# LayerNorm statistics taken block by block on ScalarE, and half of the prologue's transposes evicted by it

## What is computed

```
x = x + LN(attention(LN(x)))          # 32 query heads, 8 key/value heads, D = 128, causal
x = x + LN(ffn(LN(x)))                # base linear 4096 x 4096 + bias + 8 LoRA experts, top 2
LN(x) = (x - mean(x)) / sqrt(var(x) + 1e-5)      # over the 4096 columns
k = (LN(x) @ Wk_down.T) @ Wk_up.T     # through a latent of 256; v likewise
```

## Time and profile before

| | us |
|---|---|
| median of three runs | 4313.06 (4311.9 to 4434.4) |
| profiled execution | 4312.42 |
| its span, slowest core | 4310.7 |
| spans of the eight cores | 4282.8 to 4310.7 |
| busy: TensorE matmul, VectorE, POOL, ScalarE | 2639.9, 1227.6, 904.5, 849.7 |

### The profile page before, as it was taken

One profiled execution on the slowest core, in us unless ns is written; L12 is line 12 of the kernel. 1 busy time (PEld: TensorE's weight loads), 2 busy tenths in 40 slices (PEclk: granted clock), 3 DMA queues, 4 the chain that ended last, 5 costly groups with the idle time before them and its releaser, 6 DMA issues.

```text
span 4310.7 us, 36132 instructions; the slowest of 8 cores (4282.8 to 4310.7 us)
## 1 busy us (share of the span) xinstructions
PE 2639.9 (61%) x9712; PEld 926.6 (21%) x9902; DVE 1227.6 (28%) x1892; ACT 849.7 (20%) x1127; POOL 904.5 (21%) x1707
## 2 busy tenths in 40 slices
PE   2434628856666688218870687677778788408880
PEld 0111103311111233103320233111112133103330
DVE  2224630034554401340023101333333300340004
ACT  3230030023333200110002100444545400110001
POOL 1211004420000154104430354000000045203440
PEclk9766759977767799659985798687878799758995
DMA  9993068840000199437873997000000089636882
GB/s 193 181 218 49 6 158 122 124 56 1 1 1 1 24 127 125 86 62 109 112 99 134 171 124 108 1 1 1 1 1 1 1 120 126 95 78 91 106 110 85
DMA packets 399886, 345.53 MB, mean 80 GB/s; under 512 B 173520, under 2 KB 388688, under 8 KB 389200
## 3 DMA queue, kind: packets, MB, share of 16 engines
q0 software_dynamic: 255344, 223.54, 38.6%
q1 hardware_dynamic: 144352, 119.68, 10.0%
HBM read 516.20 MB, written 16.78 MB: 124 GB/s over the span
## 4 chain that ended last, share of the span: by engine, by line
PE 36%; DVE 20%; DMA 18%; issue 13%; ACT 7%; POOL 4%; SPq 2%; DVEq 1%; ACTq 0%; POOLq 0%
PE pb L670 6%; PE pb L846 6%; DVE recb L52 6%; DVE a L52 5%; DVE sm L52 5%; PE pb L1180 5%; PE pb L748 4%; PE pb L722 4%; PE pb L744 4%; ACT probs L52 3%; PE pb L761 3%; DMA wbuf<-wb_t 3%; DMA probs<-wb_t 2%; DMA wbuf<-wkv_t 2%; DVE x L52 2%
## 5 line engine op out<-in xcount | busy, mean ns | idle before, releaser
L52 ACT ACTIVATE probs<-pb,bvec 128x512 bf16<-128x512 f32 x768 | 527.6, 687 | 668.2 <-PE pb L722 497.9
L52 DVE CAST a<-pb 128x512 bf16<-128x512 f32 x208 | 143.8, 691 | 1644.2 <-PE pb L1188 586.0
L830 POOL DMA_DIRECT2D wbuf<-wo_t x256 | 135.3, 530 | 1527.5 <-remote 779.0
L670 PE MATMUL pb<-a,wbuf 128*128 128x512 bf16 x1003 | 258.5, 411 | 276.0 <-DMA a<-a 220.7
L744 PE MATMUL pb<-probs,V 128*128 128x512 bf16 x752 | 311.9, 415 | 101.2 <-DVE probs L52 99.7
L1180 PE MATMUL pb<-wbuf,a 128*128 128x512 bf16 x1340 | 337.4, 395 | 25.6 <-DMA wbuf<-wb_t 20.4
L52 DVE TENSOR_TENSOR probs<-probs,masks 128x512 bf16<-128x512 bf16 x512 | 217.8, 425 | 473.1 <-ACT probs L52 464.3
L52 ACT ACTIVATE x<-a 128x512 bf16<-128x512 bf16 (+1 forms) x128 | 162.5, 1269 | 827.0 <-DVE sm L52 545.7
L748 PE MATMUL pb<-probs,onesb 128*1 128x512 bf16 x768 | 317.4, 413 | 10.2 <-DVE probs L52 5.2
L722 PE MATMUL pb<-a,KT 128*128 128x512 bf16 x735 | 315.7, 429 | 4.3 <-ACT probs L52 3.7
L982 POOL DMA_DIRECT2D wbuf<-wb_t x344 | 182.5, 535 | 525.1 <-PE pb L1180 463.9
(11 more groups left out here) (92 smaller groups left out, 2400.2 us busy)
## 6 DMA issues: line engine op xcount, KB each, us to landing
wbuf<-wb_t POOLq DMA_DIRECT2D x344, 128.0 KB, 4.1
a<-x SPq DMA_DIRECT2D x32, 1024.0 KB, 7.1
wbuf<-wq_t POOLq DMA_DIRECT2D x256, 128.0 KB, 4.4
wsmall<-wq_t POOLq DMA_DIRECT2D x256, 128.0 KB, 4.4
a<-xq SPq DMA_DIRECT2D x32, 1024.0 KB, 6.9
wbuf<-wo_t POOLq DMA_DIRECT2D x256, 128.0 KB, 4.3
wsmall<-wo_t POOLq DMA_DIRECT2D x256, 128.0 KB, 4.3
probs<-wb_t POOLq DMA_DIRECT2D x168, 128.0 KB, 4.1
```

Of the source, the lines that this page charges most:

```text
L52: ins = f(*a, **k)
L670: ins = te.matmul(out=b.pb[hcl][:], lhsT=wb_[:, 128 * hcl:128 * (hcl + 1)], rhs=AP(a1t, 512 * ic, [[16384, 128], [1, 512]]), start=(ic == ...
L830: b.inc(g.dma_start(out=b.wchunk_buf(idx, 8), in_=b.wo_h[128 * hc:128 * (hc + 1), 512 * og:512 * (og + 1)]), sem, 16)
```

## The change

Three kinds of edit.

1. Statistics after the output projection and at the end of the FFN: VectorE's four sums over 4096 columns go. ScalarE, after each group of casts, runs for each of the four row blocks a Copy and a Square over the 512 new columns, each with an accumulator into a column of its own. After the last group VectorE adds the eight partial sums and the eight partial sums of squares of each row block. The outputs of the Copies and Squares are dumps, in `x2` in (iii) and in `a3` (float32) in the FFN. The Squares over 4096 columns go too. In the FFN the scratch columns move from 28 to 39 to 56 to 63 of `sm`.
2. Statistics of x3: VectorE's four sums go, and ScalarE runs for each row block a Copy and a Square over 4096 columns as soon as this block's x2 is written, with the dump in `masks`.
3. Prologue: ScalarE evicts the odd transposes of both phases and VectorE the even ones. KT and V tiles both go through `pb4` and `pb5`, with the waits that this needs.

```diff
@@ prologue, ScalarE (new; VectorE's loops skip these i)
+            for i, (t_lo, Thi, g) in enumerate(P1_):
+                if i % 2 != 1:
+                    continue
+                b.wtm(sc, f"pro:scr1:{i}")
+                psx = b.pf[i % 2]
+                srcp = AP(psx[:].tensor, 0, [[1024, 128], [32, 4], [1, 32]])
+                dstp = AP(x2t, 4096 * Thi + 512 * t_lo + 256 * (g // 2) + 4 * (g % 2),
+                          [[16384, 128], [1, 4], [8, 32]])
+                sc.copy(out=dstp, in_=srcp)
+                b.mark(f"pro:scr1e:{i}", b.s_ds)
...
+                dstp = AP(a2t, 8192 + 2048 * u + 1024 * hHi + 256 * h4 + 128 * Thi,
+                          [[16384, 128], [16, 8], [1, 16]])
+                sc.copy(out=dstp, in_=srcp)
+                b.mark(f"pro:scr2e:{i}", b.s_ds)
@@ prologue, TensorE
                 if i == 0:
+                    b.wtm(te, "pro:scr1e:62")
                     b.wtm(te, "pro:scr1e:63")
...
-                    psU = b.pb[i % 2]
+                    psU = b.pb[4 + i % 2]
...
-                    if i >= 2:
+                    if i < 2:
+                        b.wtm(te, f"pro:kte:7:{2 + i}")
+                    else:
                         b.wtm(te, f"pro:ve:{(i - 2) // 2}:{(i - 2) % 2}")
-                    psV = b.pb[2 + i % 2]
+                    psV = b.pb[4 + i % 2]
...
                 b.wtm(te, f"pro:ksq:{i}")
+                if i == 0:
+                    b.wtm(te, "pro:ve:15:0")
@@ output projection, VectorE
-            for qc in range(4):
-                v.reduce_sum(out=b.sm[:, 8 + qc:9 + qc],
-                             in_=AP(a2t, 4096 * qc, [[16384, 128], [1, 4096]]), axis=AX.X)
-            b.mark(f"{pp}o:austat", b.s_dv)
             b.wtm(v, f"{pp}o:ausq")
             for qc in range(4):
+                v.reduce_sum(out=b.sm[:, 48 + qc:49 + qc],
+                             in_=b.sm[:, 8 + 8 * qc:16 + 8 * qc], axis=AX.X)
+                v.reduce_sum(out=b.sm[:, 52 + qc:53 + qc],
+                             in_=b.stats[:, 8 * qc:8 * qc + 8], axis=AX.X)
@@ output projection, ScalarE
-            b.wtm(sc, f"{pp}o:austat")
-            for qc in range(4):
-                sc.activation(out=AP(a1t, 4096 * (qc % 2), [[16384, 128], [1, 4096]]),
-                              in_=AP(a2t, 4096 * qc, [[16384, 128], [1, 4096]]),
-                              func=AF.Square, accum_out=b.sm[:, 12 + qc:13 + qc])
+            for og in range(8):
+                b.wtm(sc, f"{pp}o:aue:{og}")
+                for qc in range(4):
+                    sl = AP(a2t, 4096 * qc + 512 * og, [[16384, 128], [1, 512]])
+                    sc.activation(out=AP(x2t, 0, [[16384, 128], [1, 512]]),
+                                  in_=sl, func=AF.Copy,
+                                  accum_out=b.sm[:, 8 + 8 * qc + og:9 + 8 * qc + og])
+                    sc.activation(out=AP(x2t, 512, [[16384, 128], [1, 512]]),
+                                  in_=sl, func=AF.Square,
+                                  accum_out=b.stats[:, 8 * qc + og:8 * qc + og + 1])
@@ FFN, VectorE and ScalarE, statistics of x3
-            for tc in range(4):
-                v.reduce_sum(out=b.sm[:, 24 + tc:25 + tc],
-                             in_=AP(x2t, 4096 * tc, [[16384, 128], [1, 4096]]), axis=AX.X)
-            b.mark(f"{pp}f:x3stat", b.s_dv)
...
-            b.wtm(sc, f"{pp}o:x2done")
+                b.wtm(sc, f"{pp}o:x2:{tc}")
+                sl = AP(x2t, 4096 * tc, [[16384, 128], [1, 4096]])
+                dmp = b.masks[:, 0:4096]
+                sc.activation(out=dmp, in_=sl, func=AF.Copy,
+                              accum_out=b.sm[:, 40 + tc:41 + tc])
+                sc.activation(out=dmp, in_=sl, func=AF.Square,
+                              accum_out=b.sm[:, 44 + tc:45 + tc])
```

More of the change, by code:

```diff
@@ L308, in _ @@
             sqr(15)
+            P1_ = [(t_lo, Thi, g) for t_lo in range(8) for Thi in range(2) for g in range(4)]
+            P2_ = [(u, Thi, hHi, h4) for u in range(4) for Thi in range(2)
+                   for hHi in range(2) for h4 in range(4)]
+            for i, (t_lo, Thi, g) in enumerate(P1_):
[8 more added lines that the diff above has]
+                b.mark(f"pro:scr1e:{i}", b.s_ds)
+            for i, (u, Thi, hHi, h4) in enumerate(P2_):
+                if (64 + i) % 2 != 1:
+                    continue
+                b.wtm(sc, f"pro:scr2:{i}")
+                psx = b.pf[(64 + i) % 2]
+                srcp = AP(psx[:].tensor, 0, [[1024, 128], [16, 8], [1, 16]])
+                dstp = AP(a2t, 8192 + 2048 * u + 1024 * hHi + 256 * h4 + 128 * Thi,
+                          [[16384, 128], [16, 8], [1, 16]])
+                sc.copy(out=dstp, in_=srcp)
+                b.mark(f"pro:scr2e:{i}", b.s_ds)
             for i in range(32):
@@ L1064, in _ @@
                 b.mark(f"{pp}f:fue:{og}", b.s_dv)
[L1065 to L1068, removed]
             b.wtm(v, f"{pp}f:fsq")
             for tc in range(4):
+                v.reduce_sum(out=b.sm[:, 48 + tc:49 + tc],
+                             in_=b.sm[:, 8 + 8 * tc:16 + 8 * tc], axis=AX.X)
+                v.reduce_sum(out=b.sm[:, 52 + tc:53 + tc],
+                             in_=b.stats[:, 8 * tc:8 * tc + 8], axis=AX.X)
+            for tc in range(4):
                 v.tensor_scalar(out=b.stats[:, 48 + 2 * tc:49 + 2 * tc],
-                                in0=b.sm[:, 24 + tc:25 + tc],
+                                in0=b.sm[:, 48 + tc:49 + tc],
                                 scalar1=1.0 / D, scalar2=None, op0=ALU.mult)
-                v.tensor_scalar(out=b.sm[:, 28 + tc:29 + tc], in0=b.sm[:, 32 + tc:33 + tc],
+                v.tensor_scalar(out=b.sm[:, 56 + tc:57 + tc], in0=b.sm[:, 52 + tc:53 + tc],
                                 scalar1=1.0 / D, scalar2=EPS, op0=ALU.mult, op1=ALU.add)
-                v.tensor_tensor(out=b.sm[:, 36 + tc:37 + tc], in0=b.stats[:, 48 + 2 * tc:49 + 2 * tc],
+                v.tensor_tensor(out=b.sm[:, 60 + tc:61 + tc], in0=b.stats[:, 48 + 2 * tc:49 + 2 * tc],
                                 in1=b.stats[:, 48 + 2 * tc:49 + 2 * tc], op=ALU.mult)
-                v.tensor_tensor(out=b.sm[:, 28 + tc:29 + tc], in0=b.sm[:, 28 + tc:29 + tc],
-                                in1=b.sm[:, 36 + tc:37 + tc], op=ALU.subtract)
+                v.tensor_tensor(out=b.sm[:, 56 + tc:57 + tc], in0=b.sm[:, 56 + tc:57 + tc],
+                                in1=b.sm[:, 60 + tc:61 + tc], op=ALU.subtract)
                 v.reciprocal(out=b.stats[:, 49 + 2 * tc:50 + 2 * tc],
-                             in_=b.sm[:, 28 + tc:29 + tc])
+                             in_=b.sm[:, 56 + tc:57 + tc])
             b.mark(f"{pp}f:fvar", b.s_dv)
@@ L1118, in _ @@
                 b.mark(f"{pp}f:sig:{tc}", b.s_ds)
[L1119 to L1123, removed]
+            for og in range(8):
+                b.wtm(sc, f"{pp}f:fue:{og}")
+                for tc in range(4):
+                    sl = AP(a2t, 4096 * tc + 512 * og, [[16384, 128], [1, 512]])
+                    sc.activation(out=AP(b.a3[:].tensor, 0, [[4096, 128], [1, 512]]),
+                                  in_=sl, func=AF.Copy,
+                                  accum_out=b.sm[:, 8 + 8 * tc + og:9 + 8 * tc + og])
+                    sc.activation(out=AP(b.a3[:].tensor, 512, [[4096, 128], [1, 512]]),
+                                  in_=sl, func=AF.Square,
+                                  accum_out=b.stats[:, 8 * tc + og:8 * tc + og + 1])
             b.mark(f"{pp}f:fsq", b.s_ds)
```

20 lines of the change are left out of this document (11 added, 9 removed).

## The result

| | before | after |
|---|---|---|
| median of the runs, us | 4311.64 (10 runs) | 4191.16 (10 runs) |
| ratio | | 0.9714, 95% interval 0.969 to 0.9737 |
| profiled execution, us | 4312.42 | 4205.09 |
| span, slowest core | 4310.7 | 4203.0 |
| median span of the eight cores | 4301.3 | 4177.3 |

The change makes the kernel 2.9% faster, 123 us by the ratio. In some executions of either kernel the cores of a die run at a lower clock and the time is some per cent longer; the medians include them, the ratio doesn't.

A forecast was written before the change was run, and what follows sets the result against it. No single engine bounds the kernel; its stages run one after another, each with its own limit. Savings of 26.2 + 25.9 + 24.6 + 24.6 + 20.6 + 2 = 123.9 us from 4312.4 gave about 4189 us, range 4165 to 4215.

The forecast's parts named there:

- What bounds the kernel: Whole kernel: no single engine; stages run one after another, so a change saves what it takes out of its stretch.
- Sites 1 to 3: Statistics after the output projection (26.2, 25.9 us saved), at the FFN's end (24.6 + 24.6) and of x3 (20.6).
- Site 4: Prologue transposes split between VectorE and ScalarE: first phase saves 6.4 us, second loses 4.2, net +2.
- the best end of my range: First transpose phase: 10.6 us saved if the scattered write pattern costs ScalarE nothing and VectorE's 1.35 us cycle stands.
- Both lengths that I named as signs: Prologue transposes: the first phase would take about 47 us and the second about 32.
- Site 5: KT and V through pb4 and pb5: at most one eviction's wait each, 0.77 us; taken as 0, other end 1.5.
- Table loads: ScalarE: Copy and Square share a table, so loads shouldn't exceed 13; 5 us lost at an end of the range.
- Exclusive scattered writes: First transpose phase: the two engines' scattered writes exclude one another, losing 9.6 us instead of gaining 6.4; 4205 us, chance 0.08.
- Loads between Copy and Square: Statistics on ScalarE: each last operation gets a 1.28 us table load, 46 us in all; 4235 us, chance 0.03.
- Time given back by the clock or the loads: TensorE's clock or load-bound stretches: 10 us a pass lost, 4209 (0.08), or a third of the gain, 4230 (0.03).
- A strided ScalarE eviction at 4.7 us: First transpose phase: the eviction length from which the change would be slower than before; slower had chance 0.01.
- its good end (4184): Whole sum: the time in us if all unknown terms came at their good end; 4160 to 4175 had chance 0.03.

The follow-up runs named there:

- the kernel with hidden work: Kernel before plus an unused ScalarE Copy and Square for each of the first seven groups' blocks (output projection, FFN), old statistics kept; ratio 0.9998.

## Why the prediction was right, point by point

| term, us saved | predicted | measured, core 0 |
|---|---|---|
| output projection, pass 0 and 1 | 26.2, 25.9 | 26.2, 25.7 |
| end of the FFN, pass 0 and 1 | 24.6, 24.6 | 24.4, 24.7 |
| x3, both passes | 20.6 | 20.7 |
| first transpose phase | 6.4 | 10.6 |
| second transpose phase | -4.2 | -0.1 |
| KT, V, norms | 0 | 0.1 (52.56 + 57.82 to 52.10 + 58.13) |
| sum | 123.9 (rounded +2 for the phases) | 132.3 |
| time, us | 4189 | 4191.16 |

*What bounds the kernel* held: with no engine the bound, each site's stretch passed to the time, one for one within a scatter of some 10 us; the stages behind started earlier and were as long as before.

*Sites 1 to 3* held to 0.3 us each. What carried them is the accumulator's repeat time of 3.80 against 3.62 us, carried over to the 512-column form (0.81 measured), and the 14.4 us pace of the x2, which hid three of four blocks. Two gaps are 9.1 rather than 8.9 because ScalarE paused once for 0.37 us among its eight operations (pass 0, end of the FFN) or began 0.43 us after the last cast in place of 0.15 (pass 1, output projection).

*Site 4* had the right mechanism and two terms off. The cycle of one tile bounds both phases, as derived from the earlier trace rows. But the adjacent ScalarE eviction is 0.267 us, not 0.34: I took it from a 512-column Activate minus 384 columns, 0.31, with an allowance for PSUM and the pointer. The allowance wasn't needed, and the Copy is another 0.04 shorter, for which no run shows the cause. And its hand-overs are 0.59, not 0.64. So its cycle is 0.86 us against VectorE's 0.85, and the second phase loses 0.1 us, not 4.2. In the first I added the pattern's 0.50 us to the base; measured, the two engines come to 723 and 726 ns, 3 apart where their adjacent forms are 43 apart. So the pattern's price isn't a surcharge on each engine's own time. The cycle is 1.34, and the best end of my range, 10.6, is what came, but not for the reason I gave that end: ScalarE does pay, but its whole scattered eviction is no longer than VectorE's. Both lengths that I named as signs, about 47 and 32 us, were missed: 43.7 and 28.6. The rule of the Trainium skill (SBUF — State Buffer, "Door 1: The DMA port swizzle"), that accesses pay for each new 16-byte line, is borne out for ScalarE too, 726 against 266 ns with only the destination changed; that both engines pay was right, how much ScalarE pays was not.

*Site 5* cost nothing, as taken.

*Table loads* stayed at 13; the one of site 1 moved under the matmuls, which is the 1.5 us between 35.07 and 33.53 in the kernel with hidden work.

*The rivals.* Exclusive scattered writes: out, by 23.4 of 27.9 us busy on both engines at once. Loads between Copy and Square: out, by the 13. Time given back by the clock or the loads: not found in ten profiles beyond a scatter of 10 us; the clock did fall in pass 1's FFN on two cores of the first profile after, but it did so in the prologue-only kernel too. The load-bound stretches grew by 1 and 4 us in the changed kernel's two profiles, not by 20. A strided ScalarE eviction at 4.7 us: 0.73.

That the time came within 2 us of 4189 is luck in part: the sum was 8.4 us too small at the sites, past what I gave as its good end (4184), and the measured median is 11 us above what the sites alone give from 4312 (4180). The two errors nearly cancel. The ratio's interval, 0.969 to 0.9737, spans 20 us and holds both 123.9 and 132. By the stage sums the sites' 132 is the change's worth.

## What to carry to other kernels

Where a reduction over a whole row waits for the last column block, take partial sums block by block on an engine that idles beside the matmuls: only the last block's operations stay on the path, and their price is the instruction's repeat time with the accumulator. Before splitting evictions between two engines, look whether the engine or the tile's cycle (eviction, hand-over, transpose, hand-over) is the bound: with two tiles the second engine gave 10.6 us in one phase and nothing in the other, while two more tiles, on top of it, gave 29 in both. A VectorE operation took 0.15 to 0.16 us on [128, 1] and 0.16 to 0.25 on [128, 4], so run such operations once for all row blocks.

## What the runs showed that I had not expected

- A scattered write costs the same on both engines, 723 and 726 ns for 128 bf16 elements 16 bytes apart, against 224 and 266 ns adjacent, and 0.73 us on each when both write without pause.
- Two 128-column transposes in a row take 0.43 us at the 0.50 clock where one takes 0.30.
- The stretch ahead of every edit, 16 blocks of x loaded, normalised and projected, had a median core of 375.6 to 382.6 us from profile to profile of kernels that are the same there.
